# Low part of the attention result between the two pairs of block transposes, and a prologue with other banks and buffers

## What is computed

```
xn  = (x - mean) / sqrt(var + 1e-5)                    # x: 4 x 1024 x 256
q, k, v = xn @ w_qkv.T                                 # 16 heads of 128
q, k = q * cos + rotate_half(q) * sin, the same for k
a   = softmax(q @ k.T / sqrt(128)) @ v                 # each head
out = x + a @ w_out.T
        + gelu(xn @ W_up + up_bias) @ W_down + down_bias
```

## Time and profile before

| what | us |
|---|---|
| median of three runs | 2530.66 (2529.3 to 2532.47) |
| profiled execution, its time | 2529.94 |
| profiled execution, span from first to last instruction | 2528.1 |
| TensorE busy | 2460.0 (97%) |
| VectorE busy | 2054.3 (81%) |
| GpSimd busy | 1833.0 (73%) |
| ScalarE busy | 1352.6 (54%) |
| mean granted TensorE clock | 0.997 of full speed |

### The profile page before, as it was taken

The page is one execution under the profiler, slowest core; times in us unless marked ns, Lnnn a source line. Parts: engine busy times, 40 slices in busy tenths (PEclk is TensorE's granted clock), DMA queues, the critical chain, the costliest instruction groups (busy, mean ns, idle before and its releaser), DMA issues. The chain is left out here.

```text
span 2528.1 us, 41987 instructions
## 1 busy us (share of the span) xinstructions
PE 2460.0 (97%) x12656; PEld 2130.2 (84%) x12656; DVE 2054.3 (81%) x3209; ACT 1352.6 (54%) x2518; POOL 1833.0 (73%) x1480
## 2 busy tenths in 40 slices
PE   5999999999999999999999999999999999999999
PEld 4888888888888888888888888888888888888788
DVE  6878879787887978788797878879787887978777
ACT  5555555555555555555555555555555555555333
POOL 5778777777877777787777778777777877777231
PEclk9999999999999999999999999999999999999999
DMA  3554555556555555546655554555565455554742
GB/s 100 144 142 119 148 130 139 133 141 169 152 147 130 140 133 141 139 118 178 160 144 132 141 139 118 146 131 157 150 170 139 119 147 130 140 133 124 213 161 67
DMA packets 233876, 354.30 MB, mean 140 GB/s; under 512 B 37856, under 2 KB 95584, under 8 KB 233696
## 3 DMA queue, kind: packets, MB, share of 16 engines
q1 hardware_dynamic: 233824, 353.72, 54.1%
HBM read 66.26 MB, written 18.87 MB: 34 GB/s over the span
## 5 line engine op out<-in xcount | busy, mean ns | idle before, releaser
L919 PE MATMUL o_ps<-keys_first,v_rows 128*128 128x256 f32 x4096 | 928.3, 380 | 3.1 <-DMA keys_first<-turned_blocks 3.1
L593 ACT ACTIVATE probs<-s_ps,neg_max 128x1024 f32<-128x1024 f32 x512 | 571.2, 1116 | 594.1 <-DVE neg_max L691 589.3
L691 DVE TENSOR_REDUCE neg_max<-s_ps 128x1 f32<-128x1024 f32 x512 | 619.3, 1217 | 295.3 <-PE s_ps L919 295.1
L919 PEld LDWEIGHTS o_ps<-keys_first,v_rows 128*128 128x128 f32 x4096 | 764.4, 190 | 103.6 <-DMA keys_first<-turned_blocks 4.5
L919 PE MATMUL s_ps<-seq_parts 128*128 128x512 f32 x3072 | 829.7, 407 | 13.5 <-ACT probs L593 8.2
L919 PEld LDWEIGHTS s_ps<-seq_parts 128*128 128x128 f32 x3072 | 576.1, 188 | 131.7 <-ACT probs L593 8.7
L470 POOL TENSOR_TENSOR rope_a<-rope_a,cos 128x512 f32<-128x512 f32 x253 | 329.1, 1301 | 480.0 <-ACT rope_b L585 480.0
L701 DVE STREAM_TRANSPOSE turned_blocks<-probs 128x512 f32<-128x512 f32 x1024 | 636.4, 678 | 19.1 <-DVE mx_q L775 3.7
L919 PE MATMUL slot_ps<-seq_parts,w_parts 128*128 128x512 f32 x1506 | 387.1, 392 | 2.0 <-DMA seq_parts<-xnt_parts 2.0
L599 ACT ACTIVATE o_hi<-o_ps 128x256 fp32r<-128x256 f32 x256 | 98.4, 384 | 477.9 <-PE o_ps L919 477.9
L473 POOL TENSOR_TENSOR seq_parts<-rope_a,rope_b 128x512 fp32r<-128x512 f32 x253 | 327.8, 1296 | 19.8
(11 more groups left out here) (106 smaller groups left out, 2171.7 us busy)
## 6 DMA issues: line engine op xcount, KB each, us to landing
keys_first<-turned_blocks SPq DMA_DIRECT2D x2048, 128.0 KB, 2.7
w_raw<-in_w_qkv SPq DMA_DIRECT2D x96, 256.0 KB, 3.2
seq_parts<-xnt_parts SPq DMA_DIRECT2D x14, 1024.0 KB, 7.6
wo_raw<-in_w_out SPq DMA_DIRECT2D x64, 128.0 KB, 2.4
y<-in_x SPq DMA_DIRECT2D x16, 256.0 KB, 3.2
ln_x<-in_x SPq DMA_DIRECT2D x16, 256.0 KB, 3.3
xnt_parts<-ln_hi SPq DMA_DIRECT2D x16, 256.0 KB, 2.7
xnt_parts<-ln_lo SPq DMA_DIRECT2D x16, 256.0 KB, 3.1
```

Source lines behind the costliest of these rows:

```text
L593: nc.scalar.activation(probs[:, k2 % 4, :], s_ps[k2 % 2][:, :], ACT.Exp, bias=neg_max[:, col:col + 1], accum_out=row_sum[:, col:col + 1]). ...
L691: nc.vector.tensor_reduce(neg_max[:, k2 % 16:k2 % 16 + 1], s_ps[k2 % 2][:, :], AXX, ALU.max, negate=True).then_inc(max_ready, 1)
L919: ins = nc.tensor.matmul(out, w, m, start=(n == 0), stop=(n == len(terms) - 1))
```

## The change

On VectorE `low_out` of chunk c-2 moves from behind both tiles' transposes to between them. In the prologue the nine projections go in another order (all of `qk0` first) and into other banks, so that TensorE waits for other copies before it writes a bank again; the rotation of `qk0` 3 moves from VectorE to GpSimd, ahead of `qk1`; and the two query groups 2 and 3 are copied into parts of `turned_blocks[:, 1]`, which is free then, in place of `rope_a`/`rope_b` and `probs`. VectorE therefore waits for `qk_ready` before it turns chunk 1. No instruction is added or taken away over the whole kernel.

```diff
@@ -138,9 +138,8 @@
                 slot_ps[:, :, :].rearrange("p a b -> p (a b)").rearrange("p (t c) -> p t c", c=DIM)]
         o_ps = pb("o_ps", [P, 512])
         w_ps = pb("w_ps", [P, 512])
-        FIRST_BANKS = [w_ps[:, :], o_ps[:, :], s_ps[1][:, 0:512], s_ps[1][:, 512:1024], slot_ps[:, 0], slot_ps[:, 1],
-                       w_ps[:, :], o_ps[:, :], s_ps[1][:, 0:512]]
-        FIRST_HELD = {6: 0, 7: 1, 8: 2}
+        FIRST_BANKS = [s_ps[1][:, 0:512], s_ps[1][:, 512:1024], w_ps[:, :], o_ps[:, :], slot_ps[:, 0], slot_ps[:, 1],
+                       w_ps[:, :], o_ps[:, :], slot_ps[:, 0]]
 
         const_loaded = sem("const_loaded")
         ident_loaded = sem("ident_loaded")
@@ -219,7 +218,8 @@
         GROUPS = {(3, 0): (0, "qk0", 0), (3, 1): (1, "qk0", 1), (4, 0): (2, "qk0", 2), (4, 1): (3, "v", 0),
                   (5, 0): (4, "qk0", 3), (6, 0): (5, "v", 1), (6, 1): (6, "v", 2), (7, 0): (7, "qk1", 0),
                   (7, 1): (8, "qk1", 1), (0, 0): (9, "qk1", 2), (0, 1): (10, "v", 3), (1, 0): (11, "qk1", 3)}
-        FIRST_GROUPS = sorted(GROUPS.values())[:9]
+        FIRST_GROUPS = [(m, *g) for m, g in enumerate((("qk0", 0), ("qk0", 1), ("qk0", 2), ("qk0", 3), ("v", 0), ("v", 1),
+                                                       ("v", 2), ("qk1", 0), ("qk1", 1)))]
 
         USED = {"qk0": 5, "v": 11, "qk1": 12}
 
@@ -453,8 +453,9 @@
 
         def rope_slot(p, m):
 
-            if isinstance(p, int) and p == 0 and m == 3:
-                return probs[:, 2, 0:HALF], probs[:, 2, HALF:SEQ]
+            if isinstance(p, int) and p == 0 and m in (2, 3):
+                first_rows = turned_blocks[:, 1].rearrange("p b j t q -> p (b j t q)")[:, (m - 2) * SEQ:(m - 1) * SEQ]
+                return first_rows[:, 0:HALF], first_rows[:, HALF:SEQ]
             return rope_a[:, m % 2, :], rope_b[:, m % 2, :]
 
         def rotate(eng, engine, p, part, n, name, before):
@@ -506,8 +507,9 @@
             wo_low(0, 0)
             pool.wait_ge(const_loaded, 32)
             rotate(pool, nc.gpsimd, 0, "qk0", 1, "pool", 0).then_inc(first_keys_pool, 1)
+            rotate(pool, nc.gpsimd, 0, "qk0", 3, "pool", 1).then_inc(qk_ready, 4)
             for n in range(2):
-                rotate(pool, nc.gpsimd, 0, "qk1", n, "pool", n + 1).then_inc(qk_ready, 1)
+                rotate(pool, nc.gpsimd, 0, "qk1", n, "pool", n + 2).then_inc(qk_ready, 1)
 
             def step(i, k, first, last):
                 if k >= 16:
@@ -531,7 +533,7 @@
                     g = group_at(k, slot, last)
                     if g and g[1] != "v":
                         p = i * 2 + g[3]
-                        rotate(pool, nc.gpsimd, p, g[1], g[2], "pool", p * 8 + qk_number(g[1], g[2]) - 3).then_inc(qk_ready, 1)
+                        rotate(pool, nc.gpsimd, p, g[1], g[2], "pool", p * 8 + qk_number(g[1], g[2]) - 2).then_inc(qk_ready, 1)
 
             steps(pool, step)
 
@@ -571,8 +573,8 @@
                     return
                 m = qk_number(part, n)
 
-                if first and m in (2, 4):
-                    act.wait_ge(first_qk_dve, m // 2)
+                if first and m == 4:
+                    act.wait_ge(first_qk_dve, 1)
                 elif first and m == 5:
                     act.wait_ge(first_keys_pool, 1)
                 elif not (first and m < 4):
@@ -695,6 +697,8 @@
 
                 if n == 0 and not (first and k < 2):
                     dve.wait_ge(keys_moved[(k - 2) % 4], chunk_moves(i, k - 2))
+                if n == 0 and first and k == 1:
+                    dve.wait_ge(qk_ready, 4)
                 dve.wait_ge(probs_ready, (i * 16 + k) * 2 + n + 1)
                 for half in range(2):
                     keys = probs[:, (2 * k + n) % 4, :].rearrange("p (j h q b) -> p h j b q", h=2, q=QUAD, b=2)[:, half]
@@ -834,9 +838,6 @@
             row_max(0, 0)
             row_max(1, 1)
 
-            dve.wait_ge(first_keys_pool, 1)
-            rotate(dve, nc.vector, 0, "qk0", 3, "dve", 2).then_inc(qk_ready, 4)
-
             def step(i, k, first, last):
                 c = i * 16 + k
                 t = c * 2
@@ -844,9 +845,10 @@
                 has_out = not (first and k < 2)
                 if not tail:
                     turn(i, k, 0, first)
-                    turn(i, k, 1, first)
                 if has_out:
                     low_out(c - 2, k % 2)
+                if not tail:
+                    turn(i, k, 1, first)
                 if (k - 1, 1) == LN_SLOT:
                     dve.wait_ge(ln_hi_ready, i + 1)
                     nc.vector.tensor_tensor(ln_lo[:, :, :], slot_ps[:, 1].rearrange("p (a b) -> p a b", a=CT),
@@ -1049,14 +1051,14 @@
                 pe.wait_ge(w_lo_ready[part], 1)
                 if m < 2:
                     pe.wait_ge(x_ready, 16 * (m + 1))
-                if m in FIRST_HELD:
-                    pe.wait_ge(rope_in, FIRST_GROUPS[FIRST_HELD[m]][2] + 1)
+                if m in (6, 7):
+                    pe.wait_ge(rope_in, m - 3)
+                if m == 8:
+                    pe.wait_ge(v_ready, 1)
                 project(part, n, bank)
             pe.wait_ge(first_qk_dve, 2)
             pe.wait_ge(first_keys_pool, 1)
             scores(0, 0, False)
-            pe.wait_ge(rope_in, 6)
-            pe.wait_ge(v_ready, 1)
             scores(1, 0, False)
 
             def step(i, k, first, last):
@@ -1093,7 +1095,9 @@
                         return
                     place, part, num, ahead = g
                     if first and k == 0:
-                        if n == 1:
+                        if n == 0:
+                            pe.wait_ge(rope_in, 6)
+                        else:
                             pe.wait_ge(v_ready, 2)
                     else:
                         bank_free(i, k, n, first, last)
```

## The result

The changed kernel takes 2512.8 us, median of six runs (2510.9 to 2515.8), against 2531.8 for six runs of the kernel before (2529.3 to 2537.0). The ratio is 0.9921, 95% interval 0.9911 to 0.9932: 0.8% or 19 us faster. The forecast was 2528.5, with 2523.5 to 2533.0 as its range and "no change" as the likeliest case. It missed by 16 us, and the range doesn't hold the time.

A forecast was written before the change was run, and what follows sets the result against it. TensorE, busy 97% of the span, was taken to set the time. 1.8 + 3.2 - 0.9 - 2.65 + 2.2 - 1.5 = 2.15 us off 2529.94 gave 2527.8, about 2528.5 as median; range 2523.5 to 2533.0.

The forecast's parts named there:

- part 1: Step loop: low_out between the transpose pairs brings o_lo 1.2 us earlier; later VectorE work keeps its time where o_hi is ready.
- Cost 0: Steps 0, 2, 13 to 15: second pair up to 3 us later, row maxima at most 0.7; no time lost.
- Gain 0.11 us ... nearly sure: Step 6: the slot's projection starts 0.11 us earlier in each of 16 rounds, 1.8 us won in all.
- the wait for `ln_lo`: Step 6: a new wait of the slot's projection on ln_lo, 0.7 to 0.9 us, 16 times.
- Steps 9 and 10: Steps 9 to 11: step 9's wait goes, partly returned later; 0.27 us in 12 rounds, 3.2 us won (0 to 6.2).
- the 0.27: Gain per round at step 11's scores: at most 0.41 us, less 0.05 of delay and 0.1 of restart.
- rival D: Slower: step 10's values product waits for keys issued 0.31 us later; 10 us lost, 2538.5 us, chance 0.05.
- GpSimd's bound at step 11: Step 11: scores need GpSimd's last rotation, ending at 1029.52 against a start at 1029.93; at most 0.41 us won.
- The load: Step 11 of three rounds: the next sequence's load lands 0.31 us later, waits near 1.5 us; -0.9 us.
- The end: Last round, end of the attention: second pair waits for o_hi, last values product comes later; -2.65 us (bounds 1.5 and 3.5).
- The prologue: Third rotation to GpSimd: scores of step 1 near 46, of step 3 near 67.95; 2.2 us won (bounds 1 and 3.5).
- The clock: Step 3 after the prologue: following 5 us idle, TensorE's clock most likely halves again; -1.5 us (bounds 0 and 2.5).

The follow-up runs named there:

- experiment 7: Kernel before, low_out behind both pairs, with rounding parts 1 to 4 moved to step 6 and part 5 to step 7: 2502.9 us, ratio 0.9880.
- experiment 8: Kernel before, low_out behind both pairs, with rounding parts 1 to 3 in step 6, 4 in step 7, 5 in step 8: 2495.8 us, ratio 0.9854.
- experiment 5: Kernel before, old order, with an unread GpSimd product of 128x178 values in step 3, delaying its rotations by 0.53 us: 2509.9 us, ratio 0.9906.
- experiment 9: Changed kernel with low_out behind both pairs again from step 10 of the last round on: 2511.0 us, ratio 0.9914 against the kernel before.
- pro_only: Kernel before with only the prologue changed, low_out still behind both pairs: 2529.9 us, ratio 0.9988.

## Why the prediction was wrong, step by step

**The step that failed** is in part 1: "Everything that VectorE does after both (the row maxima above all) keeps its time in that case", and for the steps where it doesn't, "Cost 0". The slip itself was in the prediction (row maxima up to 0.7 us later; it is 0.59 in step 3). I asked of it only whether TensorE would wait for the exponential. I didn't follow it on through ScalarE's copies to GpSimd, nor ask what runs beside GpSimd. So I took 986.16 in the earlier trace rows, the start of step 6's transposes, as given, and subtracted inside the step. In truth it depends on which small instructions meet GpSimd, and the 3.06 us fell to 0.98. With it "Gain 0.11 us ... nearly sure" became 1.63 in 14 rounds. The place where the slip begins is one that the prediction listed at cost 0: step 2, where the second pair waits 1.12 us for `o_hi`.

Given its start time the arithmetic was right. In round 0 the wait for `ln_lo` is there as forecast, 0.8 us; the transposes start 0.51 us earlier than before (2.72 for 3.23), and step 6 is 0.64 shorter, so 0.13 belong to the order, for a forecast of 0.11. What was wrong is that VectorE's lateness was a quantity of its own, and the prediction named it ("VectorE comes late out of small quantisation instructions") without asking why five instructions on 128x8 numbers take 4.85 us. Had I set the 1.0 to 1.2 us of them beside the 0.20 of the reciprocal among them, the contention would have been plain before the run.

**Steps 9 and 10**, +3.2 forecast and -2.4 found. Waits for `o_lo` went as forecast. But step 8 has rounding parts too, and the transposes of step 9 start 2.53 behind the step's start for 2.02. Here the phase was against the change: in step 10 the second scores wait 0.65 us for an exponential, and the 0.27 don't come. TensorE's timeline of steps 9, 10 and 11, against the earlier trace rows:

```profile
1005.88 1.73 PE L921 MATMUL s_ps<-seq_parts 128*128 128x512 f32 x6
...
1014.17 1.74 PE L921 MATMUL s_ps<-seq_parts 128*128 128x512 f32 x6
1016.56 1.66 PE L921 MATMUL s_ps<-seq_parts 128*128 128x512 f32 x6 [0.65 <-ACT probs L595]
...
1022.03 1.73 PE L921 MATMUL s_ps<-seq_parts 128*128 128x512 f32 x6
```

That the moved parts bring steps 9 and 10 to 8.29 and 7.80 or 7.38 (experiments 7 and 8), and that the useless instruction of experiment 5 alone leaves them at 8.91 and 7.05, fits this: it hangs on the rounding parts and their phase. The 0.5 us are nearly all in one of step 8's instructions, a TENSOR_SCALAR that takes 0.29 us in experiment 7. VectorE's timelines of the kernel before and of the change:

```profile
1010.88 0.59 DVE L799 TENSOR_SCALAR mx_q<-mx_q 128x256 f32<-128x256 f32 x1
1002.85 1.08 DVE L803 TENSOR_SCALAR mx_q<-mx_q 128x256 f32<-128x256 f32 x1
```

It ends 0.15 us after the GpSimd instruction that runs beside it, in both.

**The keys' transfers**, rival D's mechanism, decided nothing: one wait of 0.2 us between 70 and 2300. GpSimd's bound at step 11, which I held against a larger gain, is real but binds only when the exponential doesn't (experiment 7).

**The load**: 4.5 us in 3 waits, as forecast ("near 1.5 us in three places"). I priced the loss at 0.9 since I took the gain before it as lost too; with 1.5 us gained elsewhere in the round, more of it was waited away.

**The end**: 2.8 us lost for a forecast of 2.65. The closeness is partly luck, since this stretch varies by up to 2 us between kernels with one order (experiment 9). Its mechanism is in VectorE's timeline of the last step, as written down for it (the second pair waits for `o_hi`):

```profile
2371.03 0.42 DVE L717 TENSOR_TENSOR o_lo<-o_ps,o_hi 128x256 fp32r<-128x256 f32 x1 [2.25 <-ACT o_hi L601]
2371.37 1.30 DVE L705 STREAM_TRANSPOSE turned_blocks<-probs 128x512 f32<-128x512 f32 x2
```

The slow clock behind the new idle time, 1.7 us in this execution, was not in it.

**The prologue**: scores of step 1 at 46.4 for 46, of step 3 at 67.16 for 67.95, behind GpSimd without a gap. The clock fell there as forecast and cost 2.8 us in the change's execution, above the bound of 2.5, and 1.3 in those of `pro_only` and experiment 9, near the forecast of 1.5. The bound was read too low: the earlier trace rows counts the busy time of a stretch with few instructions, while step 3 keeps TensorE busy in all 6.1 us that the window after shows. `pro_only` measures 3.3 us less (2529.9 for 2533.2) where its trace has 1.3 up to step 4 (78.5 for 79.8); the rest isn't explained, and its interval reaches to 0.5.

## What to carry to other kernels

When a tiny instruction ends each time just behind its neighbour on another engine, its duration is mostly a wait and belongs to a place in time, not to the instruction; a change that shifts one of the two engines by half a microsecond can win or lose 1% that no sum over the moved instructions has in it. Follow a slip to the end of its chain through every engine, not only to the bound one, and at each engine ask what runs beside it. And before crediting a reordering, run the kernel with the order kept and the shift alone: here a useless instruction did as much, and moving the small instructions away from GpSimd did more.

## What the runs showed of the hardware

- A TENSOR_SCALAR of VectorE on 128x8 numbers that takes 0.17 us alone (`before_parts`) takes until 0.03 us after the end of the GpSimd instruction during which it starts, up to 1.29 us (`before_late56`). A RECIPROCAL of the same shape stays at 0.20 in all cases shown.
- One of them can slip in between two GpSimd instructions 0.08 us apart (974.81 to 974.89); each of a chain can lose anew. Hence 0.06 us more of delay took 1.1 us off the start of step 6's transposes, and in `before_late56` a GpSimd start at 6.879 or 6.884 us decided it from round to round.
- TensorE idle for 2.7 us at the end of the attention, and for 4.9 in the prologue, was followed in the change's execution by a stretch at a granted clock of 0.50, 3.4 and 6.8 us long. The first cost 1.7 us, the second 2.8 (from the table above). The same idle time doesn't always cost the same: step 3's stretch was 3.4 us long and cost 1.3 in `pro_only`, and 3.35 us of idle time in the change, ending at 2358.5, were followed by a clock of 1.00. Filling the idle time in the prologue with 20 matmuls kept the clock at 1.00.
